# A gated attention kernel on one core: input and tables of the local layers made during the global attention, and the division of attention placed behind the masks

## What is computed

```
xn = layernorm(x)
s  = attention(xn)            # global: 16 heads of 16, softmax over all 1024 keys, rotary q and k
g  = silu(ffn(xn))            # ffn: two layers, each of
#   h = shift_token(x); q, k, v = split(h @ wqkv); q, k = l2norm(.) * scale, rotated with xpos tables
#   o = softmax over a window of 128 and the one before it, masked; x = x + o @ wo
#   h = layernorm(shift_token(x)) * lg + lb; a, g = split(h @ w1 + b1)
#   x = x + (a * gelu(g)) @ w2 + b2
out = x + s * g
```

## Time and profile before

| | |
|---|---|
| median of 3 runs | 2305.58 us (2305.26 to 2310.74) |
| profiled execution, its own time | 2310.06 us |
| its span, first to last instruction | 2308.3 us |
| mean granted PE clock, as a share of full | 0.970 |
| second block | about 144 to 853 us |
| third block, parts W = 0 to 7 | about 853 to 1001 us |

### The profile page before, as it was taken

How to read it: one execution, slowest core, us unless ns; L and a number is a source line. 1 busy time by engine, 2 the same in 40 slices (tenths; PEclk the granted TensorE clock), 3 DMA queues, 4 the chain that set the end, 5 groups by cost and what they waited for, 6 DMA issues and landing times.

```text
span 2308.3 us, 43409 instructions
## 1 busy us (share of the span) xinstructions
PE 2197.8 (95%) x14592; PEld 1287.6 (56%) x14592; DVE 1620.2 (70%) x3785; ACT 1375.1 (60%) x2547; POOL 614.2 (27%) x493
## 2 busy tenths in 40 slices
PE   7869999999999987989999999999999999999998
PEld 4533333334333335656766766756766766766755
DVE  5767999999999936666566665656666665655635
ACT  2214888888888864645655645645655645655633
POOL 4521300000000005423333333323333233333302
PEclk9975999999999998999999999999999999999999
DMA  4575111122211112210000000000010000000122
GB/s 139 181 236 173 57 57 57 56 66 66 66 47 57 43 63 94 95 37 1 1 0 0 0 0 0 27 1 1 9 37 1 1 0 0 0 0 0 55 92 73
DMA packets 76984, 108.96 MB, mean 47 GB/s; under 512 B 14204, under 2 KB 49360, under 8 KB 76752
## 3 DMA queue, kind: packets, MB, share of 16 engines
q1 hardware_dynamic: 76864, 107.30, 14.6%
HBM read 68.74 MB, written 43.95 MB: 49 GB/s over the span
## 4 chain that ended last, share of the span: by engine, by line
PE 51%; DVE 2%; issue 1%; ACT 1%; DVEq 0%; ACTq 0%
PE ffn L1199 24%; PE l_ps_o L1157 5%; PE ring L1145 5%; PE ring L1185 4%; PE ps_v L1132 3%; PE ps_q L1132 3%; PE ps_k L1132 2%; PE ring L1169 2%; PE ring L1187 1%; DVE l_probs L1675 1%; PE ring L1188 0%; ACT k_ring L1481 0%; DVE l_probs L1687 0%; ACT l_probs L1489 0%; PE ps_k L1221 0%
## 5 line engine op out<-in xcount | busy, mean ns | idle before, releaser
L669 DVE TENSOR_REDUCE maxima<-ps_m 128x1 f32<-128x512 f32 x1024 | 629.7, 683 | 30.7 <-PE ps_m L549 26.7
L737 ACT ACTIVATE probs<-ps_st 128x1024 f32<-128x1024 f32 x512 | 521.0, 1025 | 172.0 <-PE ps_st L576 152.8
L549 PE MATMUL ps_m<-k_st,q_st 48*128 48x512 f32 x1024 | 398.2, 472 | 19.8 <-DMA k_st<-ks 15.6
L576 PE MATMUL ps_st<-q_st,k_st 50*128 50x512 f32 x1024 | 373.3, 450 | 2.3 <-DMA q_st<-max_rows 1.9
L1489 ACT ACTIVATE l_probs<-l_probs,l_neg_max 128x256 f32<-128x256 f32 x512 | 254.0, 498 | 194.8 <-DVE l_neg_max L1675 194.8
L592 PE MATMUL ps_o<-probs,v_st 128*32 128x256 f32 x4096 | 327.4, 398 | 0.1
L1675 DVE CUSTOM_DVE_ANT_1 l_probs<-ring,l_mask 128x256 f32<-128x256 f32 x384 | 140.1, 421 | 198.5 <-PE ring L1185 198.0
L576 PEld LDWEIGHTS ps_st<-q_st,k_st 50*128 50x128 f32 x1024 | 157.2, 189 | 198.4 <-issue 176.5
L1468 ACT COPY p_turned<-ring 128x512 f32<-128x512 f32 x256 | 140.4, 599 | 163.7 <-PE ring L1145 163.5
L1094 POOL TENSOR_SCALAR clipped<-sumsq 128x16 f32<-128x16 f32 x64 | 16.1, 252 | 765.7 <-DVE sumsq L1642 765.7
L549 PEld LDWEIGHTS ps_m<-k_st,q_st 48*128 48x128 f32 x1024 | 169.4, 193 | 53.0 <-DVE maxima L669 31.3
(11 more groups left out here) (192 smaller groups left out, 3879.7 us busy)
## 6 DMA issues: line engine op xcount, KB each, us to landing
qs<-split SPq DMA_DIRECT2D x16, 512.0 KB, 3.5
ks<-split SPq DMA_DIRECT2D x16, 512.0 KB, 5.1
q_st<-qs SPq DMA_DIRECT2D x64, 128.0 KB, 2.5
k_st<-ks SPq DMA_DIRECT2D x64, 128.0 KB, 3.2
o<-o_sb SPq DMA_DIRECT2D x32, 256.0 KB, 2.4
hidden<-o SPq DMA_DIRECT2D x17, 256.0 KB, 6.5
x_in<-in_L_attn_x_dram SPq DMA_DIRECT2D x8, 512.0 KB, 5.6
v<-v_sb SPq DMA_DIRECT2D x16, 256.0 KB, 4.7
```

The lines of the kernel that those rows point to most:

```text
L549: nc.tensor.matmul(bank(base, use)[:, :], q_st[u][r, qt * P:(qt + 1) * P], k_st[u][r, h * CH:(h + 1) * CH], start=True, stop=True).then_in ...
L576: mm = nc.tensor.matmul(ps_st[j][:, h * CH:(h + 1) * CH], k_st[u][r, kt * P:(kt + 1) * P], q_st[u][r, h * CH:(h + 1) * CH], start=True, st ...
L669: nc.vector.tensor_reduce(maxima[:, par, side(e), tile + e // 4, e % 2:e % 2 + 1], bank(base, k + e)[:, :], AX_X, ALU.max).then_inc(m_used, 1)
L737: nc.scalar.activation(probs[:, kt % 4, j, :], ps_st[j][:, :], ACT.Exp, scale=float(G_DIM) ** -0.5).then_inc(exp_done, 1)
```

## The change

It has three pieces.

- A class `Start` holds h, the scales and their semaphores; they are allocated before the second block, so the second block's buffers lie 9 KB further on in each partition. SP issues the loads of tables and scales after the first round of the global attention; DVE scales both layers' tables and makes h of chunk 0 at the end of its list of the second block. The third block starts without these steps.
- Since v_st now lies where the first block's results are still being stored from, POOL waits for these stores before it clears v_st. o_sb and probs change places in the allocation.
- In the parts W = 1 to 7, PE's `project_o(W - 1)` moves from between the two halves of the scores to behind the second half, and DVE's `divide(W - 1)` from in front of the masks (and of the next h) to behind both halves of them, ahead of normalisation. ACT's list stays as it was.

```diff
@@ global_attention
                 body(0, True, False)
+                st.load(sp)
                 with sp.Fori(1, ITERS - 1) as i:
...
             def _(pool):
+                for c in range(2):
+
+                    pool.wait_ge(stored[c], 16 * STORES * B)
                 for cols in (slice(0, 1), slice(1 + G_DIM, 2 * G_DIM)):
...
                 body(ITERS - 1, True)
+                for l in range(DEPTH):
+                    st.scale_tables(dve, l)
+                st.take_h(dve, 0, 0)
...
+    def load(self, sp):
+        for l in range(DEPTH):
+            sp.dma_start(self.wt.tables[l][:, :, :, :], self.xpos.rearrange("(t p) s n -> p t s n", p=P)).then_inc(self.tables_in[l], 16)
+        for s, scale in enumerate(self.scale_rows):
+            sp.dma_start(self.scales[:, :, s, :], scale.unsqueeze(0).broadcast_to([P, DEPTH, HDIM])).then_inc(self.scales_in, 16)
...
@@ local_layers, PE
                         if mid_:
                             scores(W, w, 0)
-                        if not forward and W:
-                            project_o(W - 1)
...
                             scores(W, w, 1)
+                        if not forward and W:
+                            project_o(W - 1)
                         if not forward and W == CHUNKS - 1:
                             project_o(W)
...
@@ local_layers, SP
-                load_tables(0)
-                for s, scale in enumerate((q_scale, k_scale)):
-                    sp.dma_start(scales[:, :, s, :], scale.unsqueeze(0).broadcast_to([P, DEPTH, HDIM])).then_inc(scales_in, 16)
-                load_tables(1)
...
@@ local_layers, DVE
-                        if not forward and W:
-                            divide(W - 1)
                         if next_one and not forward:
                             take_next(g, la, lf)
...
                             mask_and_max(g, w, 0)
                             mask_and_max(g, w, 1)
+                        if not forward and W:
+                            divide(W - 1)
+                        if mid_:
                             normalise(W, 0)
                             normalise(W, 1)
...
                     if l == 0:
 
-                        scale_tables(0 if name == "wqkv" else 1)
                         return
...
-                take_h(0, 0)
+                dve.wait_ge(st.tables_done, DEPTH)
```

More of the change, by code:

```diff
@@ L330, in _, with global_attention @@
                 body(B - 1, False, True)
-def global_attention(nc, wt, ident_in, qs_dram, ks_dram, v_dram, stored, o_dram, o_stored):
+def global_attention(nc, wt, st, ident_in, qs_dram, ks_dram, v_dram, stored, o_dram, o_stored):
     with ExitStack() as ctx:
@@ L354, in global_attention @@
         v_in = sb("v_in", [P, TILES, P])
+        o_sb = sb("o_sb", [P, 2, CH])
         probs = sb("probs", [P, 4, 2, L])
-        o_sb = sb("o_sb", [P, 2, CH])
         ps_st = [ps(f"ps_st{j}", [P, L]) for j in range(2)]
@@ L888, in load_small, with __init__, take_h, scale_tables @@
                 get(self.lnp[l][:, 1, :], ln_b[l].rearrange("(k p) -> p k", p=P))
-def local_layers(nc, wt, xpos, q_scale, k_scale, xnt, w_out_t, o_dram, o_stored, inv_dram, s_dram, s_stored, x, x_early, out):
+class Start:
+    def __init__(self, ctx, nc, wt, xnt, xpos, q_scale, k_scale):
+        sb = lambda n, s, d=F32: ctx.enter_context(nc.sbuf_tensor(n, s, d))
+        sem = lambda n: ctx.enter_context(nc.semaphore(n))
+        self.nc, self.wt, self.xnt, self.xpos, self.scale_rows = nc, wt, xnt, xpos, (q_scale, k_scale)
+        self.h = [sb(f"h_{n}", [P, KD, CH], F32R) for n in ("high", "low")]
+        self.scales = sb("scales", [P, DEPTH, 2, HDIM])
+        self.h_high, self.h_ready = sem("h_high"), sem("h_ready")
+        self.scales_in, self.tables_done = sem("scales_in"), sem("tables_done")
+        self.tables_in = [sem(f"tables_in{l}") for l in range(DEPTH)]
+    def load(self, sp):
[3 more added lines that the diff above has]
+            sp.dma_start(self.scales[:, :, s, :], scale.unsqueeze(0).broadcast_to([P, DEPTH, HDIM])).then_inc(self.scales_in, 16)
+    def take_h(self, dve, g, n):
+        nc, h = self.nc, self.h
+        src = lambda k, s: self.xnt[:, k, bass.ds(n, 1), s].rearrange("p o n -> p (o n)")
+        cols = (slice(1, 1 + CH), slice(0, CH))
+        for k in range(KD):
+            nc.vector.tensor_copy(h[0][:, k, :], src(k, cols[k])).then_inc(self.h_high, 1)
+        for k in range(KD):
+            dve.wait_ge(self.h_high, KD * g + k + 1)
+            nc.vector.tensor_tensor(h[1][:, k, :], src(k, cols[k]), h[0][:, k, :], ALU.subtract).then_inc(self.h_ready, 1)
+    def scale_tables(self, dve, l):
+        half = HDIM // 2
+        dve.wait_ge(self.scales_in, 16 * 2)
+        dve.wait_ge(self.tables_in[l], 16)
+        for s in range(2):
+            sc = self.scales[:, l, s, :].rearrange("p (o n) -> p o n", o=1)
+            for t, to, of in ((0, slice(0, HDIM), slice(0, HDIM)), (1, slice(0, half), slice(half, HDIM)), (1, slice(half, HDIM), slice(0, half))):
+                tab = self.wt.tables[l][:, :, 2 * s + t, to]
+                ins = self.nc.vector.tensor_tensor(tab, tab, sc[:, :, of].broadcast_to([P, TILES, to.stop - to.start]), ALU.mult)
+        ins.then_inc(self.tables_done, 1)
@@ L894, in local_layers @@
+def local_layers(nc, wt, st, xnt, w_out_t, o_dram, o_stored, inv_dram, s_dram, s_stored, x, x_early, out):
     with ExitStack() as ctx:
@@ L899, in local_layers @@
         tables, (rope_a, rope_b) = wt.tables, wt.rope
-        h = [sb(f"h_{n}", [P, KD, CH], F32R) for n in ("high", "low")]
-        scales = sb("scales", [P, DEPTH, 2, HDIM])
+        h, h_ready = st.h, st.h_ready
         v_ring = sb("v_ring", [P, WPC, INNER])
@@ L931, in local_layers @@
         mask_picked = sem("mask_picked")
[L932 to L936, removed]
         q_mm, k_mm, v_mm = sem("q_mm"), sem("k_mm"), sem("l_v_mm")
@@ L1395, in store_s @@
                     sp.dma_start(s_dram[c], s_sb[:, :, :]).then_inc(s_stored, 16)
-                load_tables = lambda l: sp.dma_start(tables[l][:, :, :, :], xpos.rearrange("(t p) s n -> p t s n", p=P)).then_inc(tables_in[l], 16)
-                load_tables(0)
-                for s, scale in enumerate((q_scale, k_scale)):
-                    sp.dma_start(scales[:, :, s, :], scale.unsqueeze(0).broadcast_to([P, DEPTH, HDIM])).then_inc(scales_in, 16)
-                load_tables(1)
                 sp.dma_start(w_out[:, :].rearrange("p (k n) -> p k n", k=KD), w_out_t.rearrange("(k p) n -> p k n", p=P)).then_inc(w_out_in, 16)
@@ L1621, in take_h @@
                         dve.wait_ge(v_mm, WPC * g)
[L1622 to L1628, removed]
+                    st.take_h(dve, g, n)
                 def rotate(g, w, la):
@@ L1937, in gated_attention_kernel @@
             prepare_tokens(nc, wt, x, w_qkv_t, rope, ident, xnt, qs_dram, ks_dram, v_dram, stored)
-            global_attention(nc, wt, ident, qs_dram, ks_dram, v_dram, stored, o_dram, o_stored)
-            local_layers(nc, wt, xpos, q_scale, k_scale, xnt, w_out_t, o_dram, o_stored, inv_dram, s_dram, s_stored, x, x_early, out)
+            st = Start(layers, nc, wt, xnt, xpos, q_scale, k_scale)
+            global_attention(nc, wt, st, ident, qs_dram, ks_dram, v_dram, stored, o_dram, o_stored)
+            local_layers(nc, wt, st, xnt, w_out_t, o_dram, o_stored, inv_dram, s_dram, s_stored, x, x_early, out)
 _INS = ['L0_attn_x', 'L0_attn_w_qkv', 'L0_attn_w_out', 'L0_ffn_wqkv', 'L0_ffn_q_scale', 'L0_ffn_k_scale', 'L0_ffn_wo', 'L0_ffn_ln_g',
```

## The result

The changed kernel takes 2339.59 us (median of 4 runs, 2335.14 to 2349.51) against 2305.42 us: ratio 1.0152, 95% interval 1.0126 to 1.0178, so slower by 35 us. Forecast were 2342 us and a range of 2326 to 2356. The profiled execution took 2335.14 us, its span is 2333.4 us.

The account below looks back on a forecast made before the run. The local layers' opening parts were taken as nearly a serial chain through PE, with about 1 us of air each. 43.8 + 0.3 - 4.5 - 3.2 gave + 36.4 us, a median of 2342 us, range 2326 to 2356.

Parts of the forecast that it names:

- Moved division and projection, order: In W = 2 to 7 the later projection delays exponentials and turning: 5.4 us a part at full clock, bounds 5.4 and 5.9.
- Clock: PE's pauses bring half clock in each changed part: 1.35 to 2.4 us more on the projection, middle 1.9.
- The full-clock case: Rival, chance 0.25: PE keeps full clock throughout, + 25.0 us, 2330.5 us, or 2328 with the larger savings.
- Six parts: W = 2 to 7 each pay 7.3 us for order and clock, 43.8 us together.
- W = 1: The division waits for its transfer there anyway, so the move costs net + 0.3 us, bounds 0 and 0.8.
- Seam: Start of the third block: early h and tables end W = 0's rotation sooner, saving 4.5 us, bounds 4.5 and 6.4.
- Second table scaling: In g = 2, part 1, its removal saves PE's pause and half clock: 3.2 us, bounds 1.9 and 3.6.
- Moved transfers and POOL's wait: Loads in SP's queue after the first round cost 0, upper bound 4 us once (chance 0.03); POOL's wait costs 0.
- Length of the global attention: Sign: the prediction is wrong if this length moves.
- Sum: 43.8 + 0.3 - 4.5 - 3.2 gives + 36.4 us over the kernel before.
- each part absorbs the delay: Rival, chance 0.04: the delayed projection costs nothing in the parts and only the savings remain, - 7.7 us, 2298 us.

Follow-up runs that it names:

- the pauses filled: Changed kernel with four extra matmuls per part, one behind the first scores and three behind the second, results overwritten: ratio 1.0104.
- the order alone: Kernel before with only the division and the projection moved, without early tables and h: ratio 1.0196.
- early start alone: Changed kernel with division and projection put back to their old places, tables and h staying early: ratio 0.9969 against the kernel before.
- h back behind the barrier: Early start kernel with h of chunk 0 made behind the barrier again, tables still early; one run, 145.28 us from barrier to g = 2.
- a second execution of the same steps: Early start kernel with the second layer's tables scaled in g = 2 again, equal up to there; one run, 140.93 us from barrier to g = 2.
- the one of the ten that gained least: Early start with new order in W = 1, copies behind exponentials there, and extra matmuls, four in W = 1, six in W = 7: ratio 0.9930.
- ACT's order changed: Changed kernel with ACT's two copies of the projection moved behind the eight exponentials: ratio 1.0148.
- Nine in place of four: Changed kernel with nine extra matmuls per part W = 1 to 7, three behind the first scores and six behind the second: ratio 1.0189.
- early start with the new order in W = 1: Early start kernel with division and projection moved in W = 1 alone, copies behind the exponentials there: ratio 0.9964 against the kernel before.
- the kernel with the division back: Changed kernel with the division in front of the masks again, projection staying behind the second scores: ratio 1.0085.

## Why the prediction was right

Point by point, with what each term measured:

- **Moved division and projection, order**: 5.4 us a part forecast, 5.5 measured (21.9 - 16.4). The times of W = 2 followed the working: projection 6.85 us after the first scores (6.97 worked out), after pauses of 1.78 and 2.81 us (1.8 and 3.0).
- **Clock**: 1.9 forecast, 2.1 measured in W = 2 with the pauses filled, 1.6 to 2.1 in W = 4 to 7. The full-clock case (chance 0.25) is out. The Trainium skill's rule on pauses that bring the half rate back in every pass ("TensorE: Matmul & The Clock Gate", section "HAM oscillation — how this bites in real kernels") is borne out for pauses shorter than those it tells of: two of 1.8 and 2.8 us with 1.1 us of work between them brought it in each part from W = 2 to 7.
- **Six parts**: 6 x 7.3 = 43.8 forecast; 188.54 - 147.29 = 41.25 in all, of which the six made 7.66, 7.80, 7.34, 7.41, 7.55 and 7.81, together 45.6.
- **W = 1**: + 0.3 forecast, + 2.6 measured. The moves themselves were sized rightly: with the order alone the part took 24.00 us in place of 24.23. Left out was how the clock of this part comes out when it starts earlier: early start alone added 1.4 us, all of it in the projection (6.44 us in place of 5.06), and the moves on top of it 1.2. The granted clock of the part was 0.86 before, 0.80 and 0.75. In the changed kernel the part ran its scores at half clock too, so that the masks ended late and the division began at 7.25 us after the first scores, in place of 6.1 as worked out; and it took 2.13 us beside POOL. The projection took 5.92 us in place of 5.06.
- **Seam**: - 4.5 taken, bounds 4.5 and 6.4; - 6.9 measured. PE did keep the full clock over its 1.6 us pause, and POOL's clearings ended 2.4 us after the barrier in place of 3.0, with DVE silent beside them; with h back behind the barrier they took 3.0 again. I had taken the wrong end, and put the other one half a microsecond short. In the early-start kernel 2.1 of the 6.9 us were lost again in W = 1 and 7, in a second execution of the same steps 0.6.
- **Second table scaling**: - 3.2 taken, - 3.3 in the changed kernel, - 2.8 in the early-start one, - 1.6 in the one of the ten that gained least. The standing alone is 1.9.
- **Moved transfers and POOL's wait**: 0 taken; the store behind them was issued at once, PE had no pause for the maximum rows behind them, and early start alone is as much faster as its stretches say.
- **Length of the global attention**: the prediction called itself wrong if this moved, and the barrier came 12.9 us earlier. It isn't the change's doing: where the full clock came at the same time, the block is as long as before (last section).
- **Sum**: + 36.4 forecast; the two stretches give + 38.0, the timed runs + 35. The errors, forecast less measured, of + 2.4 (seam), - 2.3 (W = 1) and - 1.8 (six parts) partly cancel; that the total is nearer than its terms is luck. The range's lower end, 2326, is put 2 us below the sum that it names, 2328; nothing hung on it.
- **Rivals**: "each part absorbs the delay" would have given 2298; the air of 0.5 and 1.1 us in a part was all that was absorbed. What stood against it, ACT's order, was only part of the reason: with ACT's order changed the price stays at 6.9 us in W = 2.

## What to carry to other kernels

A wait moved to a later place on one engine holds up everything behind its consumers in the other engines' lists: division and projection moved by two groups of masks cost 5.5 us a part although the division takes 1.2 us, because PE's next projection of q and k and ACT's exponentials stood behind them. In a stage where PE is busy for 94% of a part, count how far the moved step pushes PE's next one; what exceeds the air in the part is paid, in each part. A pause on PE can also cost what comes after it at half clock, here 2.1 us for 4.6 us of standing; matmuls of no use, of just the pause's length, gave that back in most parts, not in all. Nine in place of four cost 3.2 us a part.

## What the runs showed that I had not expected

The barrier's time differs by 13 us between executions, even where the second block is the same: 840.88 us in the changed kernel, 853.74 in early start with the new order in W = 1. The difference arises in this block's opening: all executions run at half clock from PE's long wait near 137 us on, and get the full clock between 194 and 224 us. Windows of PE before and changed:

```profile
190.00:200.00 10.00, 10.00 (x60) 0.50 0.82 264
200.00:210.00 10.00, 10.00 (x57) 0.50 0.45 158
```
```profile
190.00:200.00 10.00, 10.00 (x82) 0.77 0.80 268
200.00:210.00 10.00, 10.00 (x101) 1.00 0.74 245
```

The eleven profiled experiments fall in line: full clock from 198 us on and the barrier at 843.3, 202 and 844.8, 211 and 847.9, 218 and 851.8, 224 and 853.6 us. At the same time of rise, 224 us, old and new second block are equally long: the barrier came at 853.76 before and at 853.74 in early start with the new order in W = 1. So the early loads and table work cost nothing there. What decides when the clock rises, with PE busy in the records for all of the time from 190 us on, stays open. A single pair of executions can't show a change of 0.5% here; the stretches behind the barrier can.

The rate after a pause isn't the same each time either: the same 1.9 us pause in g = 2 was followed by half clock in one kernel and by full clock in another, the pause of 1.8 us in the kernel with the division back by both in one execution, and the same W = 1 took 23.3 us with the copies last throughout and 25.6 us in the version that was equal to it up to there.
